# Decoder layer on one core: block-diagonal key matrix made by GpSimd masks, context projections one group earlier, second buffers in the last group, input in three transfers

## What is computed

```python
def reference(x, ctx, ...):
    # 1. gated linear attention, 8 heads
    n = layernorm(x);  xc = silu(causal_conv4(n))
    q, kg, v, g = xc @ wq, xc @ wkg, xc @ wv, xc @ wg + bg
    gk = log_sigmoid(kg) / 16;  k = 1 - exp(gk)
    o = scan over tokens: S = S * exp(gt) + kt vt^T;  ot = (qt * scale) S
    o = o + sigmoid(sum(q * aug * k) * v);  o = normalise per head(o)
    x = x + silu(g) * o @ wout
    # 2. cross attention, 16 heads of 8
    q, k, v = layernorm(x) @ Wq.T, ctx @ Wk.T, ctx @ Wv.T
    x = x + softmax(q k^T / sqrt(8)) v @ Wo.T
    # 3. routed block: the 48 tokens of 64 with the highest router score
    n = layernorm(x);  picked = top_k(n @ w_router, 48)
    return x + where(picked, gelu(n @ w_block), n)
```

## Time and profile before

| what | us |
|---|---|
| median of 3 runs (374.22 to 376.35) | 375.64 |
| the profiled execution | 373.81 |
| its span in the trace | 372.1 |
| TensorE busy in the span | 281.2 (76%) |
| VectorE busy | 244.3 (66%) |
| ScalarE busy | 202.6 (54%) |
| GpSimd busy | 178.2 (48%) |

### The profile page before, as it was taken

The page is one execution under the profiler, slowest core; times in us unless marked ns, Lnnn a source line. Parts: engine busy times, 40 slices in busy tenths (PEclk is TensorE's granted clock), DMA queues, the critical chain, the costliest instruction groups (busy, mean ns, idle before and its releaser), DMA issues.

```text
span 372.1 us, 9366 instructions
## 1 busy us (share of the span) xinstructions
PE 281.2 (76%) x3570; PEld 199.0 (53%) x3570; DVE 244.3 (66%) x534; ACT 202.6 (54%) x342; POOL 178.2 (48%) x216
## 2 busy tenths in 40 slices
PE   0123572778989898989898989898988989869730
PEld 0002561564676567656755775677657746635520
DVE  3740554537788689868986898679866666626223
ACT  5051254236845882698459745974595367436201
...
DMA packets 17596, 12.73 MB, mean 34 GB/s; under 512 B 3856, under 2 KB 14608, under 8 KB 17552
## 3 DMA queue, kind: packets, MB, share of 16 engines
...
...
## 4 chain that ended last, share of the span: by engine, by line
PE 39%; ACT 19%; issue 13%; DVE 10%; SPq 8%; POOL 4%; DMA 1%; POOLq 0%; ACTq 0%; DVEq 0%
PE AT L679 8%; SPq L237 5%; PE S L747 5%; ACT pr L1073 5%; PE PA L696 4%; PE PT L771 4%; ACT prT L1078 4%; DVE y L1256 3%; SPq L246 3%; PE AT L618 2%; ACT L1042 2%; PE S L757 2%; PE PB L733 2%; DVE at L1302 2%; PE PB L784 2%
## 5 line engine op out<-in xcount | busy, mean ns | idle before, releaser
L1354 DVE TENSOR_REDUCE nmax<-S 128x16 bf16<-128x1024 f32 x32 | 39.1, 1222 | 37.8 <-PE S L747 37.8
L1078 ACT COPY prT<-PT 128x512 f32<-128x512 f32 x64 | 37.0, 579 | 19.9 <-PE PT L771 19.7
L771 PE MATMUL PT<-ident,pr 128*128 128x128 f32 x256 | 40.6, 281 | 8.5 <-ACT prT L1078 7.0
L458 POOL TENSOR_TENSOR kc<-ke,e_r 128x512 f32<-128x512 f32 x32 | 39.9, 1276 | 11.3 <-issue 11.3
L679 PE MATMUL AT<-q_bd,kc 128*64 128x128 f32 x512 | 34.5, 291 | 14.2 <-DVE at L1302 5.6
L784 PEld LDWEIGHTS PB<-v_x,prT 128*64 128x64 f32 x1024 | 34.9, 137 | 16.2 <-issue 12.1
L784 PE MATMUL PB<-v_x,prT 128*64 128x18 f32 x1024 | 40.9, 213 | 1.1 <-ACT prT L1078 0.3
L679 PEld LDWEIGHTS AT<-q_bd,kc 128*64 128x64 f32 x512 | 30.9, 147 | 17.4 <-issue 12.5
L771 PEld LDWEIGHTS PT<-ident,pr 128*128 128x128 f32 x256 | 27.7, 141 | 23.3 <-issue 10.9
L1073 ACT ACTIVATE pr<-S,rs 128x1024 f32<-128x1024 f32 x32 | 35.7, 1117 | 7.3 <-PE S L757 7.3
L747 PE MATMUL S<-k_bd,qT 64*64 64x512 f32 x256 | 34.8, 614 | 4.8 <-ACT pr L1073 4.0
...
## 6 DMA issues: line engine op xcount, KB each, us to landing
q_bd<-qs SPq DMA_DIRECT2D x128, 8.0 KB
...
k_bd<-kx SPq DMA_DIRECT2D x128, 16.0 KB
...
```

What stands on the lines that cost most here:

```text
L458: nc.gpsimd.tensor_tensor(kc[:, i * NCH * L:(i + 1) * NCH * L].rearrange("p (c d s) -> p c d s", c=NCH, d=NCH), kev[:, i, :, :].unsqueeze( ...
L771: last = nc.tensor.transpose(PT[:, P * p:P * p + P], pr_v[:, i % 2, P * (hp * n + p):P * (hp * n + p) + P], ident[:, :])
L1078: nc.scalar.copy(prT[:, 512 * n:512 * n + 512], PT[:, :]).then_inc(s_prT, 1)
L1354: nc.vector.tensor_reduce(nmax[:, :], cut(S, XH, L), AX.X, ALU.max, negate=True).then_inc(s_max, 1)
```

## The change

- **Key blocks.** `keys_to_blocks` is gone, with its 128 transfers and the clearing of `k_bd`. Instead `kx` has two slots, and GpSimd multiplies it by one column of 0s and 1s for each of eight blocks (`key_blocks(g, part)`, four parts of two instructions of 128x512 each).
- **Context ahead.** `context_keys(g)` and `context_values(g)` write the two banks of `S`, one step earlier for the values, and `v_x` has two slots. `x_scores(g, 0)` waits until both results of group g+1 have been copied out of `S`.
- **Last group.** In group 7 the odd tiles' scores go to `AT`, every second half's transposes to `PA0`, the odd tiles' sums to `PA1`; `nmax` and `rden` have two slots everywhere. VectorE takes over GpSimd's part in group 7's norm, ranks and final sum (`last_norm`, `last_route`, `last_ties`, `last_count`, `last_result`).
- **Start.** x arrives in three transfers: group 0, group 1, the rest; the context's first two groups and five weights are issued ahead of the rest. `q_bd` is cleared in four parts. In groups 0 and 1 half of the `q_bd` transfers are issued by ScalarE. Group 1's layer norm moves to VectorE.
- **Order.** The lists of all engines are written anew.

The diff, cut to its core:

```diff
+        WEIGHTS = [(wq_s[:, :], wq), (wkg_s[:, :], wkg), (wv_s[:, :], wv), (wg_s[:, :], wg),
+                   (bg_s[:, :], bg), (aug_s[0:DK, :], aug), (aug_s[DK:2 * DK, :], aug)]
+        KEYS = [(WkT_s[:, :], WkT), (WvT_s[:, :], WvT)]
+        LATER = [(WqT_s[:, :], WqT), (wout_s[:, :], wout), (WoT_s[:, :], WoT), (wblk_s[:, :], w_block),
+                 (wr_s[:, :], w_router)]
+
+        def s_buf(g, i):
+
+            return AT if g == NG - 1 and i % 2 else S
+
+        def pt_buf(g, n):
+
+            return PA0 if g == NG - 1 and n else PT
+
+        def pv_buf(g, i):
+
+            return PA1 if g == NG - 1 and i % 2 else PB
 
...
+                for n in range(0, NB, 2 if g < SHARED else 1):
                     sp.dma_start(q_bdv[8 * n:8 * n + 8, n, :], qs[8 * n:8 * n + 8, :]).then_inc(s_qbd, 16)
-
-            def keys_to_blocks(g):
-                sp.wait_ge(s_kx, g + 1)
-                if g == 0:
-                    sp.wait_ge(k_clear, 1)
-                if g > 1:
-                    sp.wait_ge(s_S, TPG * (g - 1))
-                for h in range(XH):
-                    sp.dma_start(k_bdv[XD * h:XD * h + XD, g % 2, h % XHG, :],
-                                 kx[XD * h:XD * h + XD, :]).then_inc(s_kbd, 16)
...
+            sp.dma_start(conv_s[:, :], conv_w).then_inc(w_conv, 16)
             load(WEIGHTS, w_in)
-            sp.dma_start(xa[:, TPG:NT, :], x_tiles[:, TPG:NT, :]).then_inc(x_rest, 16)
+            load(KEYS, w_keys)
+            load_ctx(0)
+            sp.dma_start(xa[:, TPG:2 * TPG, :], x_tiles[:, TPG:2 * TPG, :]).then_inc(x_next, 16)
+            load_ctx(1)
...
-            def clear_queries(g):
-                nc.gpsimd.memset(q_bd[:, :], 0.0).then_inc(q_clear, 1)
-
-            def clear_keys(g):
-                nc.gpsimd.memset(k_bd[:, :], 0.0).then_inc(k_clear, 1)
+            def clear_queries(g, part):
+                cols = NB * KH // QP
+                nc.gpsimd.memset(q_bd[:, cols * part:cols * part + cols], 0.0).then_inc(q_clear, 1)
+
+            def key_blocks(g, part):
+
+                pool.wait_ge(s_kx, g + 1)
+                if g == 0 and part == 0:
+                    pool.wait_ge(k_mask, 1)
+                if g > 1:
+                    pool.wait_ge(s_S, TPG * (g - 1))
+                half = kx[:, GT * (g % 2):GT * (g % 2) + GT]
+                for h in range(2 * part, 2 * part + 2):
+                    nc.gpsimd.tensor_scalar(k_bdv[:, g % 2, h, :], half, k_rows[:, h:h + 1], None,
+                                            ALU.mult).then_inc(s_kbd, 1)
...
-                clear_keys(0)
+                clear_queries(0, 0)
+                clear_queries(0, 1)
+                scale_a(1)
+                clear_queries(0, 2)
...
                 scale_b2(n)
-                if has(a):
-                    floors(a)
+                key_blocks(b, 0)
                 if has(c):
                     route(c)
+                if has(a):
+                    floors(a)
+                if has(a + 2):
+                    scale_a(a + 2)
+                if has(a):
+                    spans(a)
                 group_norm(b)
+                key_blocks(b, 1)
+                if has(a):
+                    clipped_spans(a)
                 if has(c):
                     route2(c)
-                if has(a):
+                    count(c)
+                if has(a):
+                    scaled_keys(a)
                     products(a)
-                if has(c):
-                    count(c)
-                if has(a):
-                    spans(a)
-                    scaled_keys(a)
-                    clipped_spans(a)
+                key_blocks(b, 2)
+                key_blocks(b, 3)
                 if has(a + 2):
                     center_a(a + 2)
-                    scale_a(a + 2)
                 if has(a):
                     keys(a, 0)
                     keys(a, 1)
-                    keys(a, 2)
-                    keys(a, 3)
                 if has(c):
                     result(c)
+                if has(a):
+                    keys(a, 2)
                 if has(a + 2):
                     norm_a(a + 2)
+                if has(a):
+                    keys(a, 3)
...
                     pe.wait_ge(s_qT, g + 1)
-                    pe.wait_ge(s_kbd, 16 * XH * (g + 1))
-                    pe.wait_ge(s_vx, g + 1)
+                    pe.wait_ge(s_kbd, XHG * (g + 1))
+                    pe.wait_ge(s_kx, upto(g + 2))
+                    pe.wait_ge(s_vx, upto(g + 2))
+                elif g < NG - 1:
+                    pe.wait_ge(s_exp, TPG * g + i)
+                elif i == 1:
+                    pe.wait_ge(s_at, 2 * NG)
                 else:
-                    pe.wait_ge(s_exp, TPG * g + i)
...
                     router(c)
-                if has(a):
-                    project_qk(a)
-                x_scores(n, 1)
-                if has(c):
                     ffn(c)
                 x_attend(n, 0, 0)
+                x_scores(n, 1)
+                if has(a):
+                    project_qk(a)
+                x_attend(n, 0, 1)
                 less_max(n, 1)
+                x_values(n, 0, 0)
+                x_values(n, 0, 1)
+                if has(a):
+                    project_g(a)
+                x_attend(n, 1, 0)
+                x_scores(n, 2)
                 if has(a):
                     project_v(a)
-                x_attend(n, 0, 1)
-                x_scores(n, 2)
-                x_values(n, 0, 0)
-                x_attend(n, 1, 0)
-                x_values(n, 0, 1)
-                less_max(n, 2)
-                if has(a):
-                    project_g(a)
                 x_attend(n, 1, 1)
                 x_values(n, 1, 0)
+                less_max(n, 2)
+                x_values(n, 1, 1)
+                transpose_o(b)
+                x_attend(n, 2, 0)
                 x_scores(n, 3)
-                x_attend(n, 2, 0)
-                transpose_o(b)
-                x_values(n, 1, 1)
                 x_attend(n, 2, 1)
-                less_max(n, 3)
                 if has(a + 1):
                     transpose_x(a + 1)
                 x_values(n, 2, 0)
+                less_max(n, 3)
+                x_values(n, 2, 1)
                 if has(a):
                     aug_weights(a)
-                x_values(n, 2, 1)
                 x_attend(n, 3, 0)
                 gla_out(b)
                 x_attend(n, 3, 1)
                 x_values(n, 3, 0)
                 x_values(n, 3, 1)
-                context_values(b)
+                if has(a):
+                    context_keys(a)
                 x_out(n)
                 if has(a):
-                    scores(a, 0)
+                    context_values(a)
                 x_out2(n)
                 queries(b)
                 if has(a):
+                    scores(a, 0)
...
+            def queries_to_blocks(g):
+                act.wait_ge(s_qs, g + 1)
+                act.wait_ge(s_AT, 2 * g)
+                if g == 0:
+                    act.wait_ge(q_clear, QP)
+                for n in range(1, NB, 2):
+                    nc.scalar.dma_start(q_bdv[8 * n:8 * n + 8, n, :], qs[8 * n:8 * n + 8, :]).then_inc(s_qbd, 16)
...
+            def taps(g):
+                dve.wait_ge(w_conv, 16)
+                nc.vector.tensor_scalar(conv_half[:, :], conv_s[:, :], 0.5, None, ALU.mult)
...
                 a_stats(0)
-                constants(0)
                 first_norm(0)
+                taps(0)
+                a_stats(1)
                 a_conv(0, 0)
                 a_conv(0, 1)
                 a_conv(0, 2)
                 a_conv(0, 3)
+                first_norm(1)
+                a_stats(2)
                 a_silu(0)
-                a_stats(1)
+                constants(0)
                 a_log(0)
                 a_scan(0)
...
-                a_aug(b)
-                if has(a):
-                    a_conv(a, 2)
-                    a_conv(a, 3)
                 if has(c - 1):
                     b_result(c - 1, 1)
+                if has(c):
+                    b_residual(c)
                 a_mask(b, 0)
                 if has(c):
-                    b_residual(c)
                     b_stats3(c)
+                b_stats2(n)
                 a_mask(b, 1)
-                b_stats2(n)
                 b_max(n, 0)
                 if has(a):
                     a_silu(a)
                 if has(c):
                     b_route(c)
                 a_sums(b)
+                if has(c):
+                    b_own(c)
                 a_center(b)
                 b_max(n, 1)
+                if has(c):
+                    b_ranks(c)
+                if has(a + 2):
+                    a_stats(a + 2)
                 a_squares(b)
-                if has(c):
-                    b_own(c)
-                b_max(n, 2)
+                b_weigh(n, 0)
                 if has(a):
                     a_log(a)
                     a_scan(a)
```

(23 more changed lines are left out.)

451 lines of the change are left out of this document (260 added, 191 removed).

## The result

The changed kernel took 390.11 us in the median (388.11 to 391.35) against 375.49 (374.22 to 376.35): a ratio of 1.0387, 95% interval 1.0333 to 1.0441. The forecast was 358, from 347 to 370, and faster. A few executions of a kernel come out some per cent longer at a lower granted clock, so every ratio in this document compares only the undisturbed ones with those of the kernel before in the same session, whose median was between 372.5 and 375.8 us. Kernels of different sessions are therefore compared by their ratios: 0.01 is 3.7 us. The changed kernel's profiled execution spans 389.6 us, 17.5 more than the 372.1 of before.

What follows compares the result with a forecast made beforehand. No single engine bounded the whole: TensorE bound the steps, waiting chains the head and end. 373.8 less 11.4 (head), 0.6 (steps), 3.5 (last group), 2.1 (end) gave 356.2 profiled, so 358 us in the median, range 347 to 370.

Steps and rivals of the forecast that it cites:

- the price of a key block: Full steps, GpSimd: 0.80 us per block of 128x512, so 6.4 us a step, ends 3.5 and 10.2.
- The sum of a step: Full steps: 36.2 us each, TensorE still the bound; five steps 181.0 against 179.8, 1.2 slower.
- slower than before: Rival, chance 0.08: GpSimd bounds the steps, key blocks at 1.27, 40.8 us a step, 381 us in all.
- the convolution's 2.1: Full steps, VectorE: three convolution instructions 0.7 us longer each beside GpSimd's kc, making the fourth weigh 2.1 us late.
- `result(c)` ahead of the last kc: Full steps, GpSimd's list: result waits for VectorE's copy before the last two kc; covered by about 1 us.
- Weigh late by contention: Full steps, rival, chance 0.20: weigh before x_out late by the full 2.1 us, steps 37.6, total 365 us.
- the head: Start to the first `x_scores`: terms sum to 11.4 us less, ends 7 and 14.
- the split: Head, before first scores: half of q_bd's transfers issued by ScalarE, net gain 3.4 us, ends 0 and 5.
- From qs to group 1's scores: Head, second half: 8.6 us instead of 13.0, a gain of 4.4, ends 0 and 5.
- the last group: Group 7's attention: two score buffers let the next tile's scores run early, 3.5 us less, ends 1 and 5.2.
- The end: After the last group's attention: GpSimd's work moved to VectorE, 2.1 us less, ends 1.4 and 2.8.
- The three booked edits: End: centring and scaling on VectorE 1.0 us less, rank path off GpSimd 0.45 less, yout on VectorE 0.6 less.

Runs made afterwards that it cites:

- two-input masks: Changed kernel with each key block as a two-input multiplication by the mask column broadcast over 512 columns: 383.78 us, ratio 1.0285.
- the old lists without the clearing: Kernel before with only its key transfers replaced by GpSimd key blocks in the two-operation form: 386.3 us, ratio 1.0341.
- the second pair moved: Changed kernel with two-operation key blocks and each group's second pair of blocks moved from ahead of GpSimd's products to behind them: 356.17 us, ratio 0.948.

## Why the prediction was wrong, point by point

**The failed step: the price of a key block.** I took 0.80, ends 0.43 and 1.27, from "the nearest kind", the floors. The unhindered block took 1.56 us, the mean 1.74, outside both ends. The nearest row was nearest in size and name only: the floors give the instruction two operations, the key block one, and the form sets the time. Nor was the two-input kc an upper end, as I took for granted: a two-input product of this size takes 1.04 to 1.27, one input and one operation 1.56. From 6.4 us a step the term became 8 x 1.74 = 13.9, and GpSimd's 27.4 became 34.9: that is the whole 7.5. The kernel before has no GpSimd tensor_scalar with one operation on a large tile, so no row of it could have given the price; the range had to hold that.

**The sum of a step.** The forecast let TensorE bound the step, with GpSimd's 27.4 below its 33.3. The rival *slower than before* had the mechanism that came true (GpSimd becomes the bound, half of its waits not filled) and its threshold of 39.7 was passed, with steps of 42. It got 0.08, because its price was tied to the end of 1.27, and 0.5 to 1 us more seemed excluded by it. At 381 it was still 9 us short. With the price mended, 34.9 of work and half of 15 us of waits are 42.4, the measured step. That fit is partly luck: the rival's own working puts the convolution's 2.1 on top, which would be 44.5, and those 2.1 did not come.

**`result(c)` ahead of the last kc.** I wrote "covered by about 1 us; if the copy is later, it is next". It was: VectorE waited for yout 19.6 us in all, up to 5.8 at a time. The cover was made of GpSimd's own durations, and 1 us of it can't hold when the four blocks ahead take 8.06 instead of 3.2. With two operations the four take 4.25, and the wait for yout is 2.2 in the steps.

**Weigh late by contention: not in this kernel.** I feared 1444 ns for the convolution; it was 752 in the median of after. What suffered was GpSimd (up to 2.4 us for a block of 1.56). The two-input masks show the other side, convolution at 1410. The order of starts isn't what differs. In after two convolution steps begin 0.34 us behind the start of a run of blocks and take 1.85 together. With two-input masks they begin 0.37 behind it and take 2.85:

```profile
212.28 2.85 DVE L1331 SCALAR_TENSOR_TENSOR y<-xpad,conv_half,y 128x512 f32<-128x512 f32 x2
```

And the step at 221.69 of after runs in the middle of four key blocks in 0.74, its unhindered time. The Trainium skill ("SBUF — State Buffer", Who interferes with whom) says that a VectorE instruction with two SBUF inputs contends with a GpSimd one that reads SBUF, through shared ports with an exclusive lock, and that the order of issue and not the form decides who is blocked. The runs agree that the two contend. They don't agree that the form plays no part: it decided which engine lost.

**Lower clock.** This was not a term of my sum of the steps at all. Steps at a granted clock of 0.88 and 0.96 hold 1.5 to 4.2 us of longer matmuls. In them TensorE paid for a gap of 2 us with its length and then with matmuls at the lower level behind it.

**Right in most terms: the head.** xcT began at 19.82, behind a wait of 2.29 us for x's third part, as reasoned: 0.4 earlier than before (0.5 booked). From there to the first scores it took 17.4 instead of 21.3, 3.9 less (3.4 booked for the split), so these came at 37.24 (37.6 forecast). How much the wait for x takes back shows in the old lists without the clearing: there xcT began at 14.79 and the first scores at 36.12, even with all q_bd transfers on SP. From the first scores to qs of group 1 it took 16.8 (16.7).

The term that failed in the head is the next one. From qs to group 1's scores I booked 4.4 less, and it was 0.8 less (12.2 instead of 13.0). GpSimd's eight key blocks, 12.9 us from 43.18, don't fit in "some 8 us in which it had nothing due"; group 1's spans began only at 56.05, and ScalarE's half of the q_bd transfers, which stands behind an exponent that needs them, at 57.37, 3.3 us after SP's:

```profile
57.37 5.50 ACTq L1166 DMA_DIRECT2D q_bd<-qs  x8
```

With two operations all but the first of these eight began from 55.61 on, the leg took 9.0 (8.6 forecast) and the first `x_scores` came at 69.91 instead of 72.63 (71 forecast). So the head's miss of 2 us has the same cause as the steps'. Undoing the split of q_bd cost 1.1%, 4.3 us, against the 7.8 booked (3.4 and 4.4), and 14 in the traces: the sign holds, the size isn't shown. The Trainium skill ("Trainium Kernel Development and Optimization", Key Constraints), by which several issuing engines save issue time alone, agrees with the 6.24 against 10.89.

**Right: the last group**, 3.4 against 3.5 booked. **The end**, 3.6 against 2.1. The three booked edits came out as booked: the norm 1.0 less, the rank path 0.45 less, yout and what follows it 0.7 less (yout took 0.69 on VectorE). The other 1.4 was in no term: TensorE's first two batches of the end take 0.66 and 1.16 where they took 1.11 and 2.08 before, at the higher clock level, so x begins 2.5 us after the stretch's first matmul instead of 3.9.

**Nearly right for another kernel.** With two operations a block takes 0.70 alone, about the price that I had put in. That kernel takes 363.9, which is inside the forecast's range but 6 above its middle, and 356.2 with the second pair moved. Of the 34 us from 390.1 to 356.2, 26 are the block's form and 8 came with the move of the pair.
